# VectorE sums the two rotary products of the keys, the cosine product standing in the projection's own bank

## What is computed

```python
qkv = x @ Wqkv                       # [2048, 3*1024], 16 heads of width 64
q = l2norm(q) * qs
k = l2norm(k) * ksc
q = q * cos * scale + rotate_half(q) * sin * scale
k = k * cos * inv + rotate_half(k) * sin * inv
out = local_attention(q, k, v)       # window 32, softmax
return out @ Wo
```

## Time and profile before

| | before |
|---|---|
| median of 3 runs | 2088.4 us (2085.85 to 2089.87) |
| the profiled execution | 2085.3 us, its span 2083.4 us |
| TensorE busy | 1911.9 us, 92% |
| GpSimd busy | 1670.8 us, 80% |
| ScalarE busy | 1597.1 us, 77% |
| VectorE busy | 1582.3 us, 76% |
| chain that ended last | TensorE 71%, issue 11%, GpSimd 8%, ScalarE 5%, VectorE 4% |
| GpSimd `rn`, `tsum`, `w_nat` | 384 each, mean 1658, 1275, 1045 ns |

### The profile page before, as it was taken

The page is one execution under the profiler, slowest core; times in us unless marked ns, Lnnn a source line. Parts: engine busy times, 40 slices in busy tenths (PEclk is TensorE's granted clock), DMA queues, the critical chain, the costliest instruction groups (busy, mean ns, idle before and its releaser), DMA issues.

```text
span 2083.4 us, 67375 instructions
## 1 busy us (share of the span) xinstructions
PE 1911.9 (92%) x22192; PEld 1446.7 (69%) x22192; DVE 1582.3 (76%) x4021; ACT 1597.1 (77%) x5607; POOL 1670.8 (80%) x1264
## 2 busy tenths in 40 slices
PE   6994999988999988999988999998999999999987
PEld 4662777874777774777774777774777774777773
DVE  5766888867888866788866788876788876888875
ACT  5872888875888874888884888884888884888873
POOL 3224999967999966999966999976899975999971
PEclk8995999999999999999999999999999999999999
DMA  3001212212112112111211211111211110211110
GB/s 118 12 12 27 69 46 49 56 32 68 49 45 58 48 32 71 48 45 45 58 34 49 69 46 45 45 47 40 75 49 45 45 47 20 65 46 45 45 44 21
DMA packets 44548, 99.44 MB, mean 48 GB/s; under 512 B 7344, under 2 KB 24208, under 8 KB 43504
## 3 DMA queue, kind: packets, MB, share of 16 engines
q1 hardware_dynamic: 44400, 97.59, 18.0%
HBM read 19.59 MB, written 1.05 MB: 10 GB/s over the span
## 4 chain that ended last, share of the span: by engine, by line
PE 71%; issue 11%; POOL 8%; ACT 5%; DVE 4%; DMA 0%; ACTq 0%; POOLq 0%; DVEq 0%
PE bank L1162 9%; PE bank L1175 8%; PE bank L1189 7%; PE bank L1210 7%; PE bank L1155 7%; PE bank L1191 6%; PE bank L1190 6%; PE bank L1196 6%; PE bank L1146 3%; ACT kT L533 2%; PE bank L1291 2%; POOL rn L327 2%; POOL ropeL L360 2%; POOL tsum L329 2%; PE bank L1202 2%
## 5 line engine op out<-in xcount | busy, mean ns | idle before, releaser
L327 POOL TENSOR_TENSOR rn<-n2c,half_neg 128x8 f32<-128x8 f32 x384 | 636.7, 1658 | 80.3 <-DVE n2c L807 79.6
L495 ACT ACTIVATE prob<-bank,nmax 128x96 f32<-128x96 f32 x1536 | 502.6, 352 | 131.8 <-DVE nmax L757 131.6
L329 POOL TENSOR_TENSOR tsum<-tc_,ts_ 128x512 f32<-128x512 f32 x384 | 489.6, 1275 | 0.0
L332 POOL TENSOR_TENSOR w_nat<-tsum,rn 128x512 f32<-128x512 f32 x384 | 401.3, 1045 | 37.7 <-POOL tsum L329 15.1
L800 DVE TENSOR_REDUCE n<-nat 128x8 f32<-128x512 f32 x384 | 262.3, 683 | 140.4 <-ACT nat L511 128.1
L495 ACT ACTIVATION_READ_ACCUMULATOR prob<-bank,nmax 128x1 f32 x1536 | 333.2, 217 | 0.0
L757 DVE TENSOR_REDUCE nmax<-bank 128x4 f32<-128x384 f32 x384 | 196.3, 553 | 155.4 <-PE bank L1155 147.4
L504 ACT ACTIVATE pT<-bank 96x512 f32<-96x512 f32 x384 | 230.6, 601 | 74.5 <-PE bank L1162 72.2
L1189 PE MATMUL bank<-w_hi,xs 128*128 128x512 f32 x576 | 275.7, 479 | 12.4 <-DVE ts_ L810 9.8
L1162 PE MATMUL bank<-idf,prob 128*96 128x128 f32 x1536 | 246.0, 284 | 44.1 <-ACT kT L533 28.3
L810 DVE TENSOR_TENSOR ts_<-bank,ropeL 128x256 f32<-128x256 f32 x768 | 286.1, 414 | 0.0
(11 more groups left out here) (124 smaller groups left out, 3349.2 us busy)
## 6 DMA issues: line engine op xcount, KB each, us to landing
vspace<-v_nat SPq DMA_DIRECT2D x96, 384.0 KB, 4.0
vspace<-v_nat SPq DMA_DIRECT2D x96, 256.0 KB, 3.4
vspace<-v_nat SPq DMA_DIRECT2D x95, 128.0 KB, 2.2
nat<-w_qkv SPq DMA_DIRECT2D x5, 1536.0 KB, 8.4
wo<-w_o SPq DMA_DIRECT2D x6, 512.0 KB, 3.9
w<-w SPq DMA_DIRECT2D x6, 341.0 KB, 3.1
shared<-w_qkv SPq DMA_DIRECT2D x1, 1536.0 KB, 8.6
w<-w SPq DMA_DIRECT2D x6, 192.0 KB, 3.0
```

Of the source, the lines that this page charges most:

```text
L327: nc.gpsimd.tensor_tensor(rn[:, r, :], n2c[:, r, :], half_neg[:, 0:8], ALU.pow).then_inc(pool_step, 1)
L329: nc.gpsimd.tensor_tensor(tsum[:, r, :], tc_[:, r, :], ts_[:, r, :], ALU.add).then_inc(pool_step, 1)
L332: nc.gpsimd.tensor_tensor(w_nat[:, r, :].rearrange("p (h d) -> p h d", d=D), tsum[:, r, :].rearrange("p (h d) -> p h d", d=D), rn[:, r, :] ...
L495: last = nc.scalar.activation(prob[:, 4 * b + i, :], SB[b][:, i * SPAN:(i + 1) * SPAN], ACT.Exp, bias=nmax[:, p, 8 * G + 4 * b + i:8 * G + ...
```

## The change

Key halves (j in `SUMS` = (1, 3)) get another split of the work. VectorE makes the two sine products first, then the clamp, waits for the sines, makes the cosine product with the projection's own bank as its output, waits for that, and sums bank and `ts_` into `tsum`; only then is the bank released (`pj_dve`). GpSimd no longer adds for these j; it raises its own counter by two after `rn` and goes on to `w_nat`. Query halves (j = 0, 2) keep their instructions and order. Two semaphores are new, `ts_done` and `tc_done`.

```diff
+SUMS = (1, 3)
@@ rotate (GpSimd)
-                    nc.gpsimd.tensor_tensor(rn[:, r, :], n2c[:, r, :], half_neg[:, 0:8], ALU.pow).then_inc(pool_step, 1)
+                    nc.gpsimd.tensor_tensor(rn[:, r, :], n2c[:, r, :], half_neg[:, 0:8], ALU.pow
+                                            ).then_inc(pool_step, 2 if j in SUMS else 1)
                     eng.wait_ge(pj_dve, Q + 1)
-                    nc.gpsimd.tensor_tensor(tsum[:, r, :], tc_[:, r, :], ts_[:, r, :], ALU.add).then_inc(pool_step, 1)
+                    if j not in SUMS:
+                        nc.gpsimd.tensor_tensor(tsum[:, r, :], tc_[:, r, :], ts_[:, r, :], ALU.add).then_inc(pool_step, 1)
                     eng.wait_ge(pool_step, Q * 2 + 2)
@@ rotary (VectorE)
+                def by_cosine(dst):
+                    return nc.vector.tensor_tensor(
+                        dst.rearrange(heads3, d=D), pj[:, :].rearrange(heads3, d=D),
+                        ropeL[:, k, n, :].rearrange("p (o d) -> p o d", o=1).to_broadcast([P, 8, D]), ALU.mult)
...
+                if j in SUMS:
+
+                    by_sine().then_inc(ts_done, 1)
+                    clamp()
+                    eng.wait_ge(ts_done, t * len(SUMS) + (SUMS.index(j) + 1))
+                    by_cosine(pj[:, :]).then_inc(tc_done, 1)
+                    eng.wait_ge(tc_done, t * len(SUMS) + (SUMS.index(j) + 1))
+                    nc.vector.tensor_tensor(tsum[:, r, :], pj[:, :], ts_[:, r, :], ALU.add).then_inc(pj_dve, 1)
+                else:
+                    by_cosine(tc_[:, r, :])
+                    clamp()
+                    by_sine().then_inc(pj_dve, 1)
```

More of the change, by code:

```diff
@@ L162, in build @@
         n2_ready, n2c_ready = sem("n2_ready"), sem("n2c_ready")
+        ts_done, tc_done = sem("ts_done"), sem("tc_done")
         pool_step, w_ready = sem("pool_step"), sem("w_ready")
@@ L802, in rotary @@
                 k = 2 * (j % 2)
[L803 to L814, removed]
@@ L815, in rotary, with by_sine @@
-                last.then_inc(pj_dve, 1)
+                def by_cosine(dst):
+                    return nc.vector.tensor_tensor(
+                        dst.rearrange(heads3, d=D), pj[:, :].rearrange(heads3, d=D),
+                        ropeL[:, k, n, :].rearrange("p (o d) -> p o d", o=1).to_broadcast([P, 8, D]), ALU.mult)
+                def by_sine():
+                    for a in range(2):
+                        lo, hi = a * (D // 2), (1 - a) * (D // 2)
+                        last = nc.vector.tensor_tensor(
+                            ts_[:, r, :].rearrange(heads3, d=D)[:, :, lo:lo + D // 2],
+                            pj[:, :].rearrange(heads3, d=D)[:, :, hi:hi + D // 2],
+                            ropeL[:, k + 1, n, lo:lo + D // 2].rearrange("p (o d) -> p o d", o=1
+                                                                         ).to_broadcast([P, 8, D // 2]), ALU.mult)
+                    return last
@@ new lines, in clamp @@
+                def clamp():
+                    eng.wait_ge(n2_ready, Q + 1)
+                    nc.vector.tensor_reduce(n2c[:, r, :], n2[:, r, :, :], AX.X, ALU.max).then_inc(n2c_ready, 1)
+                if j in SUMS:
[9 more added lines that the diff above has]
+                    by_sine().then_inc(pj_dve, 1)
```

## The result

The changed kernel takes 2146.9 us (median, 2144.1 to 2151.9) against 2087.1 for the kernel before: the ratio is 1.0293, 95% interval 1.0264 to 1.0322. It is slower, as forecast, by 60 us where 48 were forecast. The profiled execution took 2151.9 us, at the upper end, its span is 2150.1 us.

A forecast was written before the change was run, and what follows sets the result against it. The ring ScalarE, VectorE, TensorE was taken as the bound, with 0.21 us between bank 1's release and project 3. +0.64-0.12 = +0.52 us a tile, 8.0 per layer, +48 us over six layers gave 2136.5 us; range 2107 to 2168.

The forecast's parts named there:

- What bounds the kernel: In a tile, ScalarE, VectorE and TensorE wait in a ring; VectorE releases bank 1 only 0.21 us before project 3.
- The key step: VectorE's rotary work on a key half before its bank is released: 2.01 us grows by 0.80 to 2.81.
- The relief of 0.12 us behind `w_nat` of j=0: In each tile TensorE loses 0.12 us waiting for GpSimd's `w_nat` of j=0; the change gives it back.
- The cover of j=3: VectorE's 0.96 us wait ahead of the next tile's first maxima hides the second sum and shrinks to 0.18.
- The layer's start: The last key half is waited for directly, +0.78 us; with GpSimd ahead, +0.6 in all at the second tile's project 3.
- (a): GpSimd is the bound and the late bank costs nothing: 2063 us, faster; chance 0.10.
- (b): The key step grows by only 0.62 us and the layer-start gains are fully had: 2107 us; chance 0.10.
- (c): VectorE's input rest collides with GpSimd's `tsum`, j=3 loses its cover: 2168 us; chance 0.18 shared with a dearer step.
- What the new profile was to show: TensorE idle some 0.6 us before project 3, tile 16.7 us, GpSimd about 66%, VectorE about 82%, sum 0.69 us.

The follow-up runs named there:

- the last experiment: Against the kernel before: the new split for key half j=3 alone, only in the tile loops, with the old split between layers; 2073.7 us, ratio 0.9952.

## Why the prediction was right, and where it was off

**What bounds the kernel.** Right. The number on which the result was said to hang, 0.21 us between the bank's release and project 3, decided it. The chain after runs through exponentials, squares, key step and project 3, as shown above.

**The key step.** Forecast 2.81 us, measured 2.91 for j=1 and 2.81 for j=3 (316.06 to 318.18+0.69). The term that was too small for j=1 is the start of the cosine product: 0.23 us after the start of `n2c` (309.18-308.95), where 0.14 was taken and 0.20 was the upper end. It is 0.22 or 0.23 in 72 of the 96 steps of j=1 and 0.12 or less in the others and in all of j=3 (317.44-317.32); why, the runs do not show. In-place write and sum were right: 0.70 (0.68 taken), 0.03 to the sum, 0.69. So project 3 was late by 0.75, not 0.64. Of the 0.90 us that the step grew by, 0.60 is the sum at its usual distance and 0.30 the waits and the write into the bank: a third of what the step grew by, and yet not a cost as such, since the step of j=3 grew by 0.80 with the same waits and its tiles lose nothing.

**The relief of 0.12 us behind `w_nat` of j=0.** Wrong. I read the 0.56 us from the transposes of j=0 to the next matmuls as a wait for GpSimd because those of j=1 took 0.43. In the profile after, `w_nat` is ready early (309.52+1.04 = 310.56, the transposes start at 311.46), and it is still 311.99-311.46 = 0.53. What follows the transposes differs: 96-row matmuls after j=0, more transposes after j=1. Only 0.03 was a wait: that distance is 0.55 to 0.57 in the tiles of before and 0.52 or 0.53 in those of after. With 0.75-0.04 in place of 0.64-0.12 the sum per tile is 0.71 in place of 0.52 (the tiles' own length says 0.69); 78 tiles (13 in each layer) make 15 us of difference, of which the smaller relief is 0.08 a tile and the later project 3 0.11. The medians differ by 12 from the forecast, the spans of the two profiles by 19.

**The cover of j=3.** Right. Forecast 0.18 us left, measured 0.17 in one tile, 0.49 in the other (the one with the hardware loop's turn, 0.33 longer). It was deeper still than the idle time said, as the doubled sum showed.

**The layer's start.** 0.78 us for j=3 was forecast, and TensorE's wait grew by just that at the start of the second layer; at the next three starts it cost 1.9 us each (the last experiment). The five starts that can be compared took 38.6 us before and 46.0 after. GpSimd's relief there, which I had balanced against it, was misread. With GpSimd's sums gone TensorE waits 0.15 us for `w_nat` at the second layer's start in place of 1.33, and then 1.32 for ScalarE's `qT`: from the scores to the probabilities it is 5.99 us against 6.00. Another wait stood right behind the first. GpSimd's relief came at the layers' ends instead, which the prediction does not mention: 57.7 us for six before, 54.2 after. These two errors have opposite signs, and that they partly cancel in the total is luck.

**Rivals.** (a) GpSimd as the bound: its relief is worth some 10 us (0.9957), not 25, and project 3 is later by far more; taking the relief back changed nothing that could be measured. (b) did not come. (c) did not happen in the change, by a hair: the input's rest started at 314.47, its second half at 314.79, and GpSimd's `tsum` at 314.85 took 1.39 us in place of 1.27, that is, GpSimd came second, by 0.06 us. In three of the experiments (bank early, sum of j=1 doubled, sum behind the maxima) the order turned and the pair took 1.6 to 1.7 us; with the doubled sum that cost nothing that shows, since the tile grew by 0.61 us, no more than the sum itself. The Trainium skill's rule (SBUF — State Buffer, "Who interferes with whom") agrees with these rows in that the one that starts first keeps the other out; it does not fit `rn`, beside which the copy of the previous keys took 0.35 us (314.21, with `rn` from 313.25 to 314.89). A `rn` that starts second is held up, 2.09 us in the run with the bank released early.

**What the new profile was to show.** GpSimd at 66% (67), the sum at 0.69 and the wait before the first maxima near 0.2 us (in one tile of two) came out. VectorE was to be at 82% and is at 77, in part because the shorter copies of the previous keys were not in the sum; and GpSimd idles ahead of two of four `rn`, not of every one.

**What the clock did.** The granted clock was 1.00 in tiles of both kernels, and the lower level was granted in stretches at the layers' ends and starts; at the six ends it fell in both profiles (0.85 or 0.86 over each). The means are 0.970 before and 0.973 after, so the clock does not explain the loss.

## What to carry to other kernels

Before moving work to the engine with the lowest busy share, find what waits for that engine's next result in its queue order: here 0.9 us more ahead of a release with 0.2 us to spare cost 0.7 us a tile, the same work where the engine idled 0.96 us afterwards cost the tiles nothing, and taking work from the engine at 96% gave 10 us in 2087. Place the moved step by slack, position by position (j=3 in the loops was faster by 0.5%, j=1 slower by 2.5%), and look for the relief where the relieved queue is serial, at the ends of loops, rather than in the steady tile. A gap between two groups of matmuls is a wait only if the same pair of groups is shorter elsewhere.

## What the runs showed of the hardware

- VectorE writes a product of 128x512 into the bank that it reads in 0.70 us; into SBUF it takes 0.68 (means of 192 in the profile after: 699 and 681 ns).
- A dependent VectorE instruction behind a semaphore starts 0.73 us after the start of one of 0.70 us (309.18 to 309.91), where one without a wait starts 0.60 after one of 0.68. So the wait costs 0.11 to 0.13 us (profile after).
- A VectorE sum of two SBUF operands took 1.26 us beside a 128x512 product of GpSimd that had started first, and 0.69 beside a 128x8 power that had (the run with the bank released early); with one operand in a PSUM bank it took 0.69 beside the same product (profile after).
- The clock granted to TensorE fell to 1.2 GHz behind idle times of 2.89 to 2.94 us at all six layers' ends of before, and at three of six behind idle times of 2.04 to 2.14 us in the run with j=3 in the loops; such an end took 8.8 us in place of 7.5.
